# Fill, steady loop and drain written out call by call in an eight-batch adaLN block

## What is computed

```python
h = layernorm(x) * (1 + ca) + sa
v, gate = split(h @ W_in + b_in, 2)
y = sigmoid(gate) * ssm(v, A, C)          # h_t = sigmoid(A) * h_{t-1} + v_t, along the 1024 rows
x = x + ga * (y @ W_out + b_out)
h = layernorm(x) * (1 + cb) + sb
w = softmax(h @ gate_w + gate_b); w = w * (w >= 0.1); w = w / sum(w)   # 8 experts
x = x + gb * sum_e w[:, e] * (h @ expert_w[e] + expert_b[e])
```

## Time and profile before

| | us |
|---|---|
| median of 3 runs | 230.62 (230.43 to 231.8) |
| profiled execution, its own time | 229.9 |
| its span, first to last instruction | 227.9 |
| VectorE busy | 210.7 (92%) |
| TensorE busy | 205.3 (90%) |
| ScalarE busy | 172.8 (76%) |
| GpSimd busy | 155.7 (68%) |
| mean granted TensorE clock | 0.975 of full |

### The profile page before, as it was taken

One profiled execution on the slowest core, in us unless ns is written; L12 is line 12 of the kernel. 1 busy time (PEld: TensorE's weight loads), 2 busy tenths in 40 slices (PEclk: granted clock), 3 DMA queues, 4 the chain that ended last, 5 costly groups with the idle time before them and its releaser, 6 DMA issues.

```text
span 227.9 us, 4259 instructions
## 1 busy us (share of the span) xinstructions
PE 205.3 (90%) x1013; PEld 148.4 (65%) x1013; DVE 210.7 (92%) x776; ACT 172.8 (76%) x558; POOL 155.7 (68%) x247
## 2 busy tenths in 40 slices
PE   0996999999999999999999999999999999959820
PEld 0864867677767767676767676757677776747510
DVE  5998685999999999999999999999999999986964
ACT  6053339797988888897979797979797988878840
POOL 8673615786868778686868686868696876667380
PEclk9999999999999999999999999999999999988985
DMA  5801010101111111102030303030000101010111
GB/s 169 222 2 35 14 46 0 52 1 55 37 46 49 49 46 46 46 28 68 4 94 0 92 1 92 3 93 0 26 25 0 46 0 50 3 46 2 44 46 46
DMA packets 19217, 9.82 MB, mean 43 GB/s; under 512 B 1289, under 2 KB 19066, under 8 KB 19194
## 3 DMA queue, kind: packets, MB, share of 16 engines
q1 hardware_dynamic: 17538, 9.03, 13.7%
q10 hardware_dynamic: 1656, 0.53, 1.0%
HBM read 5.37 MB, written 4.19 MB: 42 GB/s over the span
## 4 chain that ended last, share of the span: by engine, by line
DVE 69%; issue 11%; PE 9%; ACT 7%; DMA 2%; POOL 1%; SPq 1%; DVEq 0%; ACTq 0%; POOLq 0%
DVE mix L740 10%; DVE hs L704 7%; DVE z L692 6%; DVE bn L584 5%; ACT z L485 5%; DVE bank_v L747 4%; DVE bn L577 4%; DVE x L760 4%; DVE x L721 4%; DVE var_e L609 3%; DVE mix L733 2%; DVE mean_var L595 2%; DMA x_in<-in_L_attn_x_dram 2%; DVE mean_var L597 2%; DVE bank_v L754 1%
## 5 line engine op out<-in xcount | busy, mean ns | idle before, releaser
L485 ACT ACTIVATE z<-ring,wts 128x128 f32<-128x128 f32 x448 | 123.3, 426 | 19.1 <-DVE wts L679 18.1
L376 POOL TENSOR_TENSOR z<-z 128x512 f32<-128x512 f32 x48 | 60.5, 1287 | 20.1 <-ACT z L485 20.1
L932 PE MATMUL ring<-expert_w_hi,h_hi 128*128 128x512 f32 x128 | 65.8, 514 | 1.7 <-ACT z L485 1.5
L355 POOL TENSOR_SCALAR xn<-x,neg_mean,rstd 128x128 f32<-128x128 f32 x64 | 27.7, 448 | 39.7 <-DVE rstd L636 39.7
L933 PE MATMUL ring<-expert_w_lo,h_hi 128*128 128x512 f32 x128 | 50.8, 397 | 0.0
L934 PE MATMUL ring<-expert_w_hi,h_lo 128*128 128x512 f32 x128 | 50.7, 396 | 0.0
L932 PEld LDWEIGHTS ring<-expert_w_hi,h_hi 128*128 128x128 f32 x128 | 24.6, 192 | 11.8 <-issue 9.4
L740 DVE TENSOR_REDUCE mix<-z 128x256 f32<-128x1024 f32 x16 | 31.6, 1974 | 0.3
L933 PEld LDWEIGHTS ring<-expert_w_lo,h_hi 128*128 128x128 f32 x128 | 24.6, 192 | 8.8 <-issue 6.5
L344 POOL TENSOR_SCALAR xn<-x_in,neg_mean,rstd 128x128 f32<-128x128 f32 x64 | 28.0, 451 | 2.9 <-DVE rstd L636 2.9
L934 PEld LDWEIGHTS ring<-expert_w_hi,h_lo 128*128 128x128 f32 x128 | 24.3, 190 | 5.6
(11 more groups left out here) (115 smaller groups left out, 373.5 us busy)
## 6 DMA issues: line engine op xcount, KB each, us to landing
x_in<-in_L_attn_x_dram SPq DMA_DIRECT2D x16, 256.0 KB, 2.7
out_dram<-x SPq DMA_DIRECT2D x16, 256.0 KB, 2.3
expert_w<-in_L_ffn_expert_w_dram ACTq DMA_DIRECT2D x2, 256.0 KB, 4.2
wmod<-in_L_wmod_dram SPq DMA_DIRECT2D x1, 384.0 KB, 3.4
expert_b<-in_L_ffn_expert_b_dram SPq DMA_DIRECT2D x12, 4.0 KB
w_in<-in_L_attn_W_in_dram SPq DMA_DIRECT2D x1, 128.0 KB, 3.7
w_out<-in_L_attn_W_out_dram SPq DMA_DIRECT2D x1, 64.0 KB, 4.3
cond<-in_L_c_dram SPq DMA_DIRECT2D x1, 4.0 KB
```

The lines of the kernel that those rows point to most:

```text
L355: last = nc.gpsimd.tensor_scalar(tile(xn2, g % 2, j), tile(x1, g % SLOTS, j), neg_mean[:, g % 2, j:j + 1], rstd[:, g % 2, j:j + 1], ALU.ad ...
L376: nc.gpsimd.tensor_tensor(z[:, g % 2, t, 0:4, :], z[:, g % 2, t, 0:4, :], z[:, g % 2, t, 4:8, :], ALU.add).then_inc(folded, 1)
L485: last = nc.scalar.activation(z[:, g % 2, t, e, :], bank_k[:, (e % 4) * P:(e % 4 + 1) * P], ACT.Copy, scale=wts[:, g % 2, t, e:e + 1])
L932: mm(bank_k[:, :], hi, expert_w_hi[:, cols], start=True, stop=False)
```

## The change

Nothing of the arithmetic of a group is changed but what is listed here.

- The loop over s is replaced on every engine. The first groups and the last are written out call by call, each engine in an order of its own; in between, a loop over s = 2 to 11 (VectorE: 2 to 10) has a new order in its body. The halves go through the ring of four banks in one written order (`ring_order`), every fourth half to the same bank, and a half waits for the one four places ahead of it.
- `first_norm(0)`, `first_norm(1)` and `second_norm(0)` move from GpSimd to VectorE, with the same four instructions each.
- Of group 15, halves 1, 3, 5 and 7 are weighed by VectorE (`weigh_onto`), halves 0, 2, 4 and 6 by ScalarE, and GpSimd folds nothing of it. VectorE sums it with `fold_pairs` (128x512) and `sum_pairs` for each pair of tiles, and adds bias, scales and adds x1 in two halves of 128x256 (`last_bias`, `last_times_gb`, `last_result`), each stored by itself (`store_last`).
- The bias product comes last in PSUM, behind the main product, in `state_input` and `output_product`. The gate bias in `logits` becomes one rounded matmul of 33 rows (`gate_b_parts`) in place of an unrounded one of 1 row.
- At the start the loads of `cond` and `b_v_row` go from SyncE's queue to ScalarE's, so that the first load of x is SyncE's first; ScalarE's `pick_rows` come behind its other transfers; GpSimd's memsets change places, and its splitting of the bias rows comes behind `gab`. `keep_clock` makes 8, 4 and 6 matmuls, before 8, 8, 10 and 6.

```diff
-            for s in range(-5, groups + 1):
-                on(router, s, 2)
-                on_pair(root, s + 1, 2)
...
+            for s in range(2, 11):
+                root(s + 1, 2)
+                weigh_onto(s - 1, 7, 0)
+                root(s + 1, 3)
+                router(s, 5)
...
+                x1_stats(s + 2)
+                sum_pairs(s - 1, 0)
+                low_part(s + 1)
+                router(s + 1, 0)
+                add_bias(s - 1)
...
@@
-            for s in range(-3, groups + 1):
-                on(fold, s - 1, 1)
-                on(fold, s - 1, 2)
-                on(second_norm, s + 1)
-                on(add_pairs, s - 1)
-                on(first_norm, s + 3)
-                on(weight_parts, s)
-                on(fold, s, 0)
...
+            for s in range(2, 12):
+                add_pairs(s - 1, 0)
+                first_norm(s + 3)
+                weight_parts(s)
+                fold(s, 2)
+                fold(s, 1)
+                second_norm(s + 2)
+                fold(s, 0)
...
@@
+            for s in range(2, 12):
+                weigh(s - 1, 2)
+                exponentials(s)
+                weigh(s - 1, 6)
+                h1(s + 2)
+                weigh(s - 1, 1)
+                parts_out(s - 1)
+                weigh(s, 3)
+                gate(s + 2)
+                weigh(s, 5)
+                h2_high(s + 1)
+                weigh(s, 0)
+                h2(s + 1)
+                weigh(s, 4)
...
@@
+            for s in range(2, 12):
+                half(s - 1, 1)
+                turn_xn1(s + 2, s + 1)
+                turn_parts(s - 1, s + 1)
+                half(s - 1, 7)
+                half(s, 3)
+                half(s, 5)
+                state_input(s + 2, s - 2)
+                gate_input(s + 2, s - 1)
+                half(s, 0)
+                half(s, 4)
+                turn_xn2(s + 1)
+                output_product(s + 2)
+                half(s, 2)
+                half(s, 6)
+                mixed_bias(s - 1, s + 2)
+                logits(s + 1)
...
@@
-                mm(bank_v[:, :], b_v_parts[:, :], ones[:, :], start=True, stop=False)
-                mm(bank_v[:, :], w_in[:, 0:P], h1_t[:, g % 2, :], start=False,
-                   stop=True).then_inc(v_ready, 1)
...
+                mm(bank_v[:, :], w_in[:, 0:P], h1_t[:, g % 2, :], start=True, stop=False)
+                mm(bank_v[:, :], b_v_parts[:, :], ones[:, :], start=False, stop=True).then_inc(v_ready, 1)
```

More of the change, by code:

```diff
@@ new lines, in _ @@
+            negated_mean(0)
+            root(0, 6)
+            root(0, 7)
+            second_norm(0)
+            x_stats(4, 0)
+            first_residual(1)
+            x_stats(3, 3)
+            x_stats(4, 1)
+            x1_stats(1)
+            moments(1)
+            root(1, 0)
+            low_part(0)
+            root(1, 1)
+            negated_mean(1)
+            router(0, 0)
+            router(0, 1)
+            root(1, 2)
+            root(1, 3)
+            root(1, 4)
+            router(0, 2)
@@ new lines, in _ @@
+            scan(3)
+            router(1, 5)
+            x_stats(6, 0)
+            router(1, 6)
+            gated(3)
+            router(1, 7)
+            x_stats(6, 1)
+            sum_fours(0, 1)
+            first_residual(3)
+            x_stats(6, 2)
+            x_stats(6, 3)
+            x1_stats(3)
+            sum_pairs(0, 0)
+            low_part(2)
+            router(2, 0)
+            add_bias(0)
+            router(2, 1)
+            times_gb(0)
+            moments(3)
+            router(2, 2)
@@ new lines, in _ @@
+            x1_stats(13)
+            sum_pairs(10, 0)
+            low_part(12)
+            router(12, 0)
+            add_bias(10)
+            router(12, 1)
+            times_gb(10)
+            moments(13)
+            result(10)
+            weigh_onto(11, 7, 0)
+            weigh_onto(11, 7, 1)
+            root(13, 0)
+            weigh_onto(11, 7, 2)
+            root(13, 1)
+            router(12, 2)
+            root(13, 2)
+            router(12, 3)
+            root(13, 3)
+            router(12, 4)
@@ new lines, in _ @@
+            root(13, 4)
+            root(13, 5)
+            router(12, 5)
+            negated_mean(13)
+            root(13, 6)
+            router(12, 6)
+            root(13, 7)
+            router(12, 7)
+            weigh_onto(11, 7, 3)
+            scan(14)
+            gated(14)
+            sum_fours(11, 1)
+            first_residual(14)
+            x1_stats(14)
+            moments(14)
+            low_part(13)
+            root(14, 0)
+            sum_pairs(11, 0)
+            router(13, 0)
@@ L817, in _ @@
+            weigh_onto(15, 5, 3)
+            weigh_onto(15, 7, 3)
+            result(14)
+            fold_pairs(15, 1)
+            sum_pairs(15, 0)
+            sum_pairs(15, 1)
+            last_bias(0)
+            last_bias(1)
+            last_times_gb(0)
+            last_times_gb(1)
+            last_result(0)
+            last_result(1)
         @block.tensor
@@ new lines, in _ @@
+            half(0, 6)
+            half(0, 2)
+            half(0, 7)
+            turn_xn2(1)
+            output_product(2)
+            turn_parts(0, 2)
+            half(0, 0)
+            turn_xn1(3, 2)
+            logits(1)
+            half(0, 5)
+            half(0, 4)
+            state_input(3)
+            gate_input(3, 0)
+            half(0, 1)
+            half(1, 4)
+            half(1, 0)
+            half(1, 5)
+            output_product(3)
+            turn_xn2(2)
+            half(1, 3)
@@ new lines, in _ @@
+            turn_parts(12, 14)
+            half(13, 2)
+            gate_input(15, 12)
+            state_input(15, 11)
+            half(13, 6)
+            half(13, 5)
+            turn_xn2(14)
+            half(13, 3)
+            output_product(15)
+            half(13, 0)
+            logits(14)
+            turn_parts(13, 15)
+            half(13, 7)
+            half(13, 4)
+            mixed_bias(12, 15)
+            half(13, 1)
+            half(14, 6)
+            half(14, 2)
+            turn_xn2(15)
```

947 lines of the change are left out of this document (710 added, 237 removed), and 3 rows, old and new, of the table LAST_HALVES.

## The result

The changed kernel takes 228.06 us (median of 4, 227.88 to 228.16), the kernel before 230.53 (median of 4, 229.99 to 231.8) on the same chip: a ratio of 0.988, 95% interval 0.985 to 0.991. The forecast was 223.8. The profiled execution took 228.16, its span is 226.4.

What follows compares the result with a forecast made beforehand. VectorE was taken to bound the loop, TensorE close behind. Terms -2.0 - 1.4 + 0.2 - 3.1 - 0.2 = -6.5 gave 223.4 from the profiled 229.9, 224.1 against the median; forecast 223.8, range 218 to 229.5 us.

Steps and rivals of the forecast that it cites:

- The loop, -2.0: Nine loop steps: a step falls from 11.98 to 11.75 us as `var_e` no longer waits, -2.0 us.
- the port wait: VectorE instructions reading SBUF wait for a GpSimd fold's end, up to 1.26 us; 0.27 for `var_e` in a loop step.
- the rival of port waits: Loop: `low_part` comes behind fold 2 and waits 1.26 us each step, 11.3 more, 235.1 us; chance 0.08.
- it counts only if TensorE becomes the bound: Shorter gate bias in `logits`: about 0.2 us less TensorE work each step, covered by VectorE's bound.
- Bias order, 0: Bias matmuls last in PSUM: the same matmuls behind the same wait, so 0.
- The fill, -1.4: Start to the loop at 56.1: first weights 1.0 us later, then 2.4 less to the loop, -1.4 us.
- Pre-scan +0.2: Loop end to the scan of group 15: port waits go, logits(12) come 0.7 late; 26.1 for 25.9, +0.2 us.
- drain -3.1: Scan of group 15 to VectorE's last end: 32.3 for 35.4 us, -3.1.
- The store: Behind the last VectorE instruction: half the bytes to store, -0.2 us, from 0 to -0.6.
- Fill and drain give nothing: Rival: chains through all engines set fill and drain; the loop's -2.0 and a little remain, 227.5 us; chance 0.16.
- All in step: Rival: the fill's +1.0 and the new waits of fill and drain don't come, 219.6 us; chance 0.13.
- the likeliest case: The forecast case for the whole kernel, 220.5 to 226 us; chance 0.57.

Runs made afterwards that it cites:

- run 4: The changed kernel with the gate bias of the logits again as one unrounded matmul of 1 row: 230.91 us, ratio 0.997.
- run 11: The changed kernel with added clock matmuls at three waits of TensorE in the fill, and the gate bias matmul left out of `logits`: 226.01 us, ratio 0.978.
- run 7: The changed kernel with added clock matmuls at two waits in the fill, and the bias matmul first in `state_input` and `output_product`: 226.79 to 230.46 us, ratio 0.986.
- run 6: The kernel before with none of its clock matmuls, nothing else changed: 239.1 us against 230.8, ratio 1.028.
- run 12: The changed kernel with clock matmuls sized to the waits: 14 ahead of `turn_xn1(0)`, 8 ahead of `output_product(1)`, 2 ahead of `logits(0)`: 225.06 us, ratio 0.975.
- run 13: The changed kernel with another order of the fill on its engines, and 5, 2, 4, 5 and 1 clock matmuls: 222.87 us, ratio 0.967.
- run 3: The changed kernel with only half 7 of group 15 on VectorE; ScalarE weighs halves 1, 3 and 5, GpSimd folds tiles 0 to 2: 227.93 us, ratio 0.985.

## Why the prediction was right or wrong

**The loop, -2.0, near in size by luck, wrong in its reason.** 11.81 for 11.75, or -1.5 us in nine steps. `var_e` takes 0.16 us in the steps and `low_part` 0.68, so the port wait is gone and the rival of port waits did not occur; GpSimd and VectorE in one step:

```profile
91.54 0.68 DVE L938 TENSOR_TENSOR h_lo<-h_t,h_hi 128x512 fp32r<-128x512 f32 x1
...
94.82 0.16 DVE L821 TENSOR_SCALAR var_e<-mean_var 128x8 f32<-128x8 f32 x1
...
91.81 2.81 POOL L443 TENSOR_TENSOR z<-z 128x512 f32<-128x512 f32 x2 [0.47 <-ACT z L593]
```

`low_part` starts 0.27 us ahead of the folds; I had put 0.2. The two folds take 2.81 instead of two times 1.28, so this time the fold seems to be the one held up. But with TensorE's old gate bias the step would be 11.95 (run 4). With that bias, moving VectorE off the port waits gave only 0.05; then TensorE bound the loop, and the term that I put at nothing, "it counts only if TensorE becomes the bound", gave 0.13 of the 0.18. I had "about 11.5 us of work" for TensorE in a step; it has 11.8 (106.09 in 106.29), and the earlier trace rows already gave 105.98 / 9 = 11.78. The 0.02 of run 11 places VectorE's floor at 11.79.

**Bias order, 0: wrong, by 0.10 a step** (run 7). Both matmuls stand behind the same wait, as I argued, and their order still showed; the cause is open. If the 0.10 and the 0.13 add up, which no run shows, the new order of instructions with both old bias forms would give a step of 12.04, and the loop's gain would be the two bias edits alone.

**The fill, -1.4: wrong, +3.4.** The step that failed is the sentence "The matmuls for the clock in the fill cost nothing there: they stand before waits, and the granted clock is 1.00 in all of it with or without their neighbours busy". It took the 1.00 of the earlier trace rows, a mean over 33 us, as given whatever TensorE does, where it was the work of those matmuls: without them the kernel before loses 6.6 us of its fill (run 6). The changed kernel has fewer of them and opens holes where it has none. Closing them by length gives 3.1 of the 4.8 us (run 12). The other 1.7 I read from the traces, without a run of their own: about half behind the first weights, where VectorE is idle for 1.9 us and I had put 1.4 of new waits, and the rest ahead of them. There the normalised input was 1.3 late (13.7 for 12.4), of which `first_norm(0)` itself, 1.43 us for 1.1, is 0.3. At the start VectorE's casts of `pick_bf` stand beside GpSimd's memsets (two in 2.51 us, before three in 2.62; the memset of `pick` takes 1.49, before 0.94), and the silu of the condition stands behind two of the casts (5.01, before 2.68). With bridges the first weights stood at 35.05, 0.75 behind my 34.3. That the new chain could be shortened by 2.3 us more is run 13's; it was no part of the forecast.

**Pre-scan +0.2 and drain -3.1: right in size.** 25.8 and 32.3 us. But run 3 shows that it did not matter who weighs group 15: what I charged for "12 z blocks to VectorE" and credited for "ScalarE three halves less" cancels. The -3.1 comes ahead of group 14's long reduction, in which the second norm and the router of group 15 come earlier: from the scan of group 15 to its `wts` it is 18.5 us (191.61 to 210.12), before 21.4 (189.76 to 211.16; I had written 20), and to that reduction 19.5 for 23.3. Behind it the changed kernel takes 12.8 us, the one before 12.1 (213.03 to 225.16). Of the waits that I had listed, VectorE's last of any size is 0.74 us for logits(15), where I had 0.9. The store: -0.2, as said.

**The rivals.** "Fill and drain give nothing" (227.5) is the nearest number, and for another reason: the drain gave all of its 3.1 and the fill took 3.4 back. "All in step" (219.6) did not come. The range held the time; the likeliest case did not. That the time still fell below the one before is owed to the loop and the drain.
